# Cross-attention and quantized FFN on one core: scores and skip on fp16 pairs instead of fp32r pairs, with the scaling this needs

## The reference, cut to what matters

```python
def ln(x):                       # over the 1024 positions of a channel
    return (x - mean(x)) / sqrt(var(x) + 1e-5)
def xattn(u, c):                 # u: 128x1024, c: 128x256
    q, k, v = Wq @ u, Wk @ c, Wv @ c
    p = softmax(q.T @ k / sqrt(128))         # 1024 x 256
    return Wskip @ u + v @ p.T               # 128 x 1024
def ffn(u):                      # w: 1024x1024 from 4-bit weights
    return u @ w + bias
x = x + xattn(ln(x), ctx)
x = x + ffn(ln(x))
```

## Time and profile before

| | us |
|---|---|
| median of the three timed runs | 526.82 (526.39 to 528.74) |
| the profiled execution, its own time | 526.57 |
| its span in the trace | 524.6 |
| PE busy | 496.9 |
| POOL busy | 470.8 |
| DVE busy | 427.5 |
| ACT busy | 372.7 |

### The profile page before, as it was taken

The page is one execution under the profiler, slowest core; times in us unless marked ns, Lnnn a source line. Parts: engine busy times, 40 slices in busy tenths (PEclk is TensorE's granted clock), DMA queues, the critical chain, the costliest instruction groups (busy, mean ns, idle before and its releaser), DMA issues.

```text
span 524.6 us, 9213 instructions
## 1 busy us (share of the span) xinstructions
PE 496.9 (95%) x2668; PEld 302.8 (58%) x2668; DVE 427.5 (82%) x981; ACT 372.7 (71%) x844; POOL 470.8 (90%) x717
## 2 busy tenths in 40 slices
...
DMA packets 227059, 92.65 MB, mean 177 GB/s; under 512 B 209472, under 2 KB 214080, under 8 KB 227008
## 3 DMA queue, kind: packets, MB, share of 16 engines
...
q10 hardware_dynamic: 720, 0.14, 0.1%
...
## 4 chain that ended last, share of the span: by engine, by line
PE 86%; POOL 7%; DVE 2%; DMA 2%; issue 1%; ACT 1%; POOLq 0%; SPq 0%
PE ps_y L924 41%; PE ps_e L889 15%; PE ps_o L919 14%; PE ps_o L915 8%; PE ps_kv L900 3%; PE ps_y L928 3%; PE ps_kv L902 2%; POOL sb_prob L255 2%; POOL sb_xc_lo L270 1%; DMA sb_xnt_lo<-sb_xn_lo 1%; DMA sb_x<-in_x_dram 1%; POOL sb_xn_lo L302 1%; ACT sb_prob L480 1%; DVE sb_st L596 0%; ACT sb_wf L512 0%
## 5 line engine op out<-in xcount | busy, mean ns | idle before, releaser
L924 PE MATMUL ps_y<-sb_wf,sb_xnt_hi 128*128 128x512 f16 x512 | 192.1, 380 | 4.4 <-DMA sb_xnt_lo<-sb_xn_lo 3.4
L924 PE MATMUL ps_y<-sb_wf,sb_xnt_lo 128*128 128x512 f16 x512 | 192.0, 379 | 0.0
L480 ACT ACTIVATE sb_prob<-ps_e,sb_neg_max 128x256 f32<-128x256 f32 x256 | 118.3, 470 | 57.2 <-DVE sb_neg_max L659 57.2
L255 POOL TENSOR_SCALAR sb_prob<-sb_prob,sb_rsum 128x256 f32<-128x256 f32 x256 | 122.7, 492 | 15.2 <-DVE sb_rsum L664 15.0
L668 DVE TENSOR_TENSOR sb_p_lo<-sb_prob,sb_p_hi 128x1024 f16<-128x1024 f32 x64 | 78.3, 1223 | 48.8 <-ACT sb_p_hi L489 48.8
L889 PE MATMUL ps_e<-sb_k_hi,sb_xc_hi 128*128 128x256 f32 x256 | 90.8, 355 | 10.4 <-DVE sb_k_lo L647 5.7
L249 POOL TENSOR_TENSOR sb_o<-sb_prod,sb_x 128x512 f32<-128x512 f32 x63 | 80.6, 1279 | 7.0 <-DVE sb_prod L702 7.0
L924 PEld LDWEIGHTS ps_y<-sb_wf,sb_xnt_hi 128*128 128x128 f16 x512 | 49.9, 98 | 63.8 <-DMA sb_xnt_lo<-sb_xn_lo 4.3
L659 DVE TENSOR_REDUCE sb_neg_max<-ps_e 128x2 f32<-128x512 f32 x128 | 84.8, 681 | 1.6 <-PE ps_e L889 1.2
L924 PEld LDWEIGHTS ps_y<-sb_wf,sb_xnt_lo 128*128 128x128 f16 x512 | 50.0, 98 | 56.7
L489 ACT ACTIVATE sb_p_hi<-sb_prob 128x1024 f16<-128x1024 f32 x64 | 67.4, 1053 | 19.8 <-issue 15.5
...
## 6 DMA issues: line engine op xcount, KB each, us to landing
...
sb_pt_hi<-sb_p_hi SPq DMA_TRANSPOSE x64, 3.0
sb_pt_lo<-sb_p_lo SPq DMA_TRANSPOSE x64, 2.8
...
sb_xnt_hi<-sb_xn_hi SPq DMA_TRANSPOSE x32, 2.8
```

The lines of the kernel that those rows point to most:

```text
L255: last = pool.tensor_scalar(prob[:, j, t, :], prob[:, j, t, :], rsum[:, j, t:t + 1], P_SCALE, ALU.mult, ALU.mult)
L480: done = act.activation(prob[:, j, t, :], ps_e[j % 2][:, t, :], ACT.Exp, bias=neg_max[:, j, t:t + 1], accum_out=esum[:, j, t:t + 1])
L924: pe.matmul(ps_y[h][:, :], xnt_p[s][:, q % 2, kt, :], wf[:, kt, h * HALF:(h + 1) * HALF], start=kt == 0 and s == 0, stop=False)
```

## The change

It does this:

- The pairs of the scores and of the skip product become fp16 (`xc`, `k`, `wsk`). fp16 needs operands in range, so the first layernorm is applied in full, scaled to 1024: `inverse_std1` on POOL gets a second operation behind the power, `nb1` = -mean x inverse deviation, and ACT's `centre` uses `nb1` and `rstd1` as bias and scale pointers.
- The keys get a scale per batch: a second one-column matmul (`bound`) beside the one for the values gives a bound on the keys; DVE's `range_scales` makes both scales in three operations in place of the four of `value_scale`, and waits for the one-column matmuls instead of the key and value matmuls behind them.
- The key scale has to come out of the scores: `exps` gets a small ACT operation ahead of each chunk (`neg_top`, the row maxima times the scale, two elements per partition) for which the exponentials wait, and the exponentials get a scale pointer beside the bias pointer that they have.
- In the run-in the norms of the weights take one more reduction on DVE, the scaling of the weights moves from DVE to POOL, `key_bound` is added on DVE, the first `centre` is done in halves behind `nb1`, and `centre(1)` moves behind the exponentials of two chunks.

```diff
-        xc_hi, xc_lo = (sb(n, [P, 3, N], F32R) for n in ("xc_hi", "xc_lo"))
-        k_hi, k_lo = (sb(n, [P, 2, M], F32R) for n in ("k_hi", "k_lo"))
+        xc_hi, xc_lo = (sb(n, [P, 3, N], F16) for n in ("xc_hi", "xc_lo"))
+        k_hi, k_lo = (sb(n, [P, 2, M], F16) for n in ("k_hi", "k_lo"))
-        wsk_hi, wsk_lo = (sb(n, [C, 3, C], F32R) for n in ("wsk_hi", "wsk_lo"))
+        wsk_hi, wsk_lo = (sb(n, [C, 3, C], F16) for n in ("wsk_hi", "wsk_lo"))
...
             def inverse_std1(m):
                 pool.wait_ge(ve1_done, m + 1)
-                if ran(m, 2):
-                    pool.wait_ge(kvlo_done, m - 1)
-                pool.tensor_tensor(rstd1[:, m % 2:m % 2 + 1], ve1[:, :], neg_half[:, :],
-                                   ALU.pow).then_inc(rstd1_done, 1)
+                if ran(m, 1):
+                    pool.wait_ge(xc_done, m)
+                pool.tensor_tensor(rstd1[:, :], ve1[:, :], neg_half[:, :], ALU.pow).then_inc(rstd1_done, 1)
+                pool.wait_ge(rstd1_done, m + 1)
+                pool.tensor_scalar(nb1[:, :], mv1[:, 0:1], rstd1[:, :], -1.0, ALU.mult,
+                                   ALU.mult).then_inc(nb1_done, 1)
...
             def centre(n):
-                act.wait_ge(mv1_done, n + 1)
+                act.wait_ge(nb1_done, n + 1)
                 if ran(n, 1):
                     act.wait_ge(xclo_done, n)
-                act.activation(xc[:, :], x_sb[:, n % 4, :], ACT.Identity, bias=mv1[:, 0:1],
-                               scale=-1.0).then_inc(xc_done, 1)
+                act.activation(xc[:, :], x_sb[:, n % 4, :], ACT.Identity, bias=nb1[:, :],
+                               scale=rstd1[:, :]).then_inc(xc_done, 1)
...
             def exps(b, j):
                 act.wait_ge(max_done[j], b + 1)
                 if ran(b, 1):
                     act.wait_ge(plo_done[j // 2], b)
+                top = t_scale[:, b % 3, 1:2]
+                act.activation(neg_top[:, j, :], neg_max[:, j, :], ACT.Copy, scale=top).then_inc(top_done, 1)
+                act.wait_ge(top_done, CHUNKS * b + j + 1)
                 for t in range(TPC):
-                    done = act.activation(prob[:, j, t, :], ps_e[j % 2][:, t, :], ACT.Exp,
-                                          bias=neg_max[:, j, t:t + 1], accum_out=esum[:, j, t:t + 1])
+                    done = act.activation(prob[:, j, t, :], ps_e[j % 2][:, t, :], ACT.Exp, scale=top,
+                                          bias=neg_top[:, j, t:t + 1], accum_out=esum[:, j, t:t + 1])
                 done.then_inc(exp_done[j], 1)
...
             def run_in():
-                centre(0)
+                first_centre(0)
                 first_centred_hi(0)
                 keys_hi(0)
+                first_centre(1)
                 first_centred_hi(1)
                 keep_projections()
-                centre(1)
                 exps(0, 0)
                 exps(0, 1)
+                centre(1)
                 centred_hi(1)
...
-            def value_scale(n):
-                dve.wait_ge(kv_done, n + 1)
-                dve.tensor_scalar(t_scale[:, :], ps_m[:, HALF - 1:HALF], TINY, 1.0 / V_TOP, ALU.max,
-                                  ALU.mult).then_inc(t_step, 1)
-                dve.wait_ge(t_step, 4 * n + 1)
-                dve.reciprocal(v_scale[:, :], t_scale[:, :]).then_inc(t_step, 1)
-                dve.tensor_scalar(o_scale[:, n % 3:n % 3 + 1], t_scale[:, :], w_inv[:, :], None,
-                                  ALU.mult).then_inc(t_step, 1)
-                dve.wait_ge(t_step, 4 * n + 3)
-                dve.wait_ge(rstd1_done, n + 1)
-                dve.tensor_scalar(sk_scale[:, :], v_scale[:, :], rstd1[:, n % 2:n % 2 + 1], P_SCALE, ALU.mult,
+            def range_scales(n):
+                dve.wait_ge(bound_done, n + 1)
+                if n == 0:
+                    dve.wait_ge(floors_made, 2)
+                    dve.wait_ge(w_step, 5)
+                t = t_scale[:, n % 3, :]
+                dve.tensor_tensor(t, (ps_o[0] if n == 0 else ps_m)[:, HALF - 2:HALF], floors[:, :],
+                                  ALU.max).then_inc(t_step, 1)
+                dve.wait_ge(t_step, 3 * n + 1)
+                dve.reciprocal(t_inv[:, n % 2, :], t).then_inc(t_step, 1)
+                dve.tensor_scalar(o_scale[:, n % 3:n % 3 + 1], t_scale[:, n % 3, 0:1], w_inv[:, :], None,
                                   ALU.mult).then_inc(t_step, 1)
...
+            def bound(n, to):
+                pe.wait_ge(amax_done, n + 1)
+                peak = amax[:, n % 2:n % 2 + 1]
+                pe.matmul(to[:, HALF - 2:HALF - 1], top_inv[:, :], peak, start=True, stop=True)
+                pe.matmul(to[:, HALF - 1:HALF], kmax_row[:, :], peak, start=True, stop=True).then_inc(bound_done, 1)
...
             def keys_values(n):
                 pe.wait_ge(ctx_loaded[n % 2], nth(n, 2))
-                pe.wait_ge(amax_done, n + 1)
                 if ran(n, 1):
                     pe.wait_ge(kvlo_done, n)
-                pe.matmul(ps_m[:, HALF - 1:HALF], ones[:, :], amax[:, n % 2:n % 2 + 1], start=True, stop=True)
                 if n > 1:
+                    bound(n, ps_m)
                     pe.matmul(ps_kv[:, 0:M], proj[:, KEY, :], ctx_sb[:, n % 2, :], start=True, stop=True)
```

More of the change, by code:

```diff
@@ L97, in xattn_ffn_program @@
         mv1, mv2 = (sb(n, [P, 2]) for n in ("mv1", "mv2"))
-        rstd1 = sb("rstd1", [P, 2])
-        ve1, ve2, rstd2, nb2, rs2 = (sb(n, [P, 1]) for n in ("ve1", "ve2", "rstd2", "nb2", "rs2"))
+        ve1, rstd1, nb1, ve2, rstd2, nb2, rs2 = (sb(n, [P, 1]) for n in ("ve1", "rstd1", "nb1", "ve2", "rstd2", "nb2", "rs2"))
         ps_e = [pb(f"e{k}", [P, TPC, M]) for k in range(2)]
@@ L269, in centred_lo @@
                 cols = slice(h * HALF, (h + 1) * HALF)
-                last = pool.tensor_tensor(xc_lo[:, n % 3, cols], xc[:, cols], xc_hi[:, n % 3, cols].bitcast(F32),
+                last = pool.tensor_tensor(xc_lo[:, n % 3, cols], xc[:, cols], xc_hi[:, n % 3, cols],
                                           ALU.subtract)
@@ L364, in run_in @@
                 inverse_std1(0)
+                scale_weights()
                 zero_point_quotient()
```

111 lines of the change are left out of this document (65 added, 46 removed).

## The result

The changed kernel takes 550.96 us (median of 4 runs, 550.40 to 552.34) against 527.57 for the kernel before beside it (526.39 to 528.74): 1.045 times as long, 95% interval 1.041 to 1.048. The forecast said slower, at 543 with an upper end of 551; the measured time stands at that end. The profiled execution took 551.24, its span is 549.3.

What follows compares the result with a forecast made beforehand. It took PE to set the 15.22 us step, with a DVE, POOL and ACT loop close behind that would grow to 15.7. From 526.57 us, +13.4 for 28 steps, +2.5 run-in, +0.5 end: 543; range 522 to 551.

Steps and rivals of the forecast that it cites:

- the run-in: Start of the kernel, up to the FFN's start: 2.5 us longer, between 1 and 4.
- The step was right, 15.7: Steady step per batch: grows from 15.22 to 15.7 us, 28 times, +13.4 us in all.
- the ring: DVE, POOL and ACT waiting on each other in turn, from one `probs_lo(b, 1)` to the next: 15.22 us before the change.
- the loop: The same cycle through DVE, POOL and ACT: 14.91 us without PE, forecast at 15.45 to 15.95 after the change.
- the 0.31 us wait: DVE at `value_scale`, waiting for PE's key and value matmuls: the cycle's only slack, gone after the change.
- the middle that I took: 15.7 us a step, between 15.91 if `probs_lo(b, 0)` goes before `nb2` and about 15.5 if `nb2` goes first.
- The small costs: Per chunk on ACT, 0.31 us for the small operation and 0.18 for pointers on two exponentials; score matmuls at 0.108.
- The lock: A two-input DVE instruction and a POOL one reading SBUF exclude each other; the first to issue delays the other.
- PE's saving arrives: Rival: ACT's added costs are at most 0.1 us a chunk, PE's 14.92 us step holds, 521 us; chance 0.18.
- POOL becomes the bound: Rival: `nb1` costs 0.75 us and `xc_lo` gains nothing, step 16.2 or more, 557 us; chance 0.07.
- The last steps: End of the kernel: the last step's cycle adds 0.5 us.

Runs made afterwards that it cites:

- `wait_only`: The kernel before with POOL's product of mean and inverse deviation added and ACT's centring waiting for it, result unused: 533.90 us, ratio 1.012.
- `no_top`: The changed kernel without the small ACT operation and without the exponentials' scale pointer, softmax of unscaled scores: 521.39 us, ratio 0.988.
- `hi_first`: The changed kernel with POOL's third-batch power moved earlier, chunk 3 normalised before the second layernorm, and ACT's `probs_hi(b, 1)` before `apply_norm2`: 557.28 us, ratio 1.057.
- `dve_top`: The changed kernel with the scaled row maximum made on DVE instead of ACT, and POOL's third-batch power ahead of the zero-point remainder: 583.58 us, ratio 1.105.
- `halves_only`: The kernel before with only the score and skip pairs in fp16, unscaled, so low halves keep fewer digits: 516.16 us, ratio 0.979.
- `power_first`: The changed kernel with POOL's power and product for the third batch moved ahead of the zero-point remainder: 547.48 us, ratio 1.038.

## Why the forecast was right and wrong

**The step that failed is the run-in**: "1.1 + 2 x 0.49 + some 0.4", 2.5 us where 9.0 came: 6.5 of the 8 us that the forecast lacks. I counted that the first keys wait for the power and the product, and that the second centring stands behind two longer chunks. I did not follow the new wait to the third batch, whose power stands on POOL behind the zero-point work, and I took from the earlier trace rows that POOL had no gap there, when the change itself makes gaps: ACT waits for POOL (2.87 us), and POOL then for ACT's exponentials (2.99, the row at 31.82). `wait_only` shows 6.2 us for the wait by itself in the kernel before. In `no_top`, without the costs on ACT, the run-in is 5.2 us longer than before (first `sb_o` row at 61.74), so ACT's costs have 3.8 of the 9.0, where I had 2 x 0.49. The granted clock of TensorE is low in stretches of both run-ins (0.50 from 35 to 40 us before, 0.54 from 45 to 50 us after); what that costs there, no run shows.

**The step was right, 15.7, but partly by luck.** The row maxima of chunks 1 and 2 start 5.03 us into the ring (412.57 to 417.60), not 5.37: the loop held more slack than the 0.31 us wait that I took for all of it, and without PE and ACT's costs it takes about 14.4, where my terms make 14.7 (14.91 less the 0.2 saved on DVE). Of this lead 0.20 us is left at `probs_lo(b, 0)`, 11.92 us into the ring (396.84 to 408.76) for 12.12. And the two instructions did not split the difference: `probs_lo(b, 0)` went first, which I had priced at 15.91. Less 0.20, that is the 15.71 measured; the middle that I took is the same number for another reason. By the `sb_o` rows the step before is 15.18 and not 15.22, so the 28 steps cost 14.8 us for 13.4.

**The small costs held.** The small operation takes 0.29 us (0.30 forecast), an exponential 0.56 where it took 0.47 (0.088 forecast), score matmuls 0.109 apart (0.108). The profile has a mean of 560 ns for the exponential after and 470 before. The Trainium skill's page ScalarE: Activation LUTs, section What ACT_TABLE_LOAD costs, prices a pointer at 93 ns; the 90 ns here agree. PE's waits ahead of chunk 3's scores are 0.31 to 0.61 us in the steady steps, 0.61 in about half of them; I had asked for 0.6 or more.

**The lock** decides as the forecast's reading of the Trainium skill's page SBUF — State Buffer, section Who interferes with whom, had it: the two exclude each other and the first to issue keeps the other waiting. The trace agrees for `nb2`, which ends 0.12 to 0.14 us after the low half in the kernel before, the changed kernel and the three that lack one or both costs. POOL first, which the earlier trace rows did not have, is now shown: `hi_first` has the low half 0.80 us longer behind a sum that had started 0.34 us earlier, and `dve_top` has an operation of two elements, with one tile and a pointer for inputs, held to the end of a POOL instruction that had started 0.10 or 0.29 us earlier. It is not so for every pair. POOL's power on one element starts 0.06 us ahead of the low half in the kernel before (403.33),

```profile
403.27 0.55 POOL L279 TENSOR_TENSOR sb_rstd<-sb_ve,sb_neg_half 128x1 f32<-128x1 f32 x1
```

and neither holds up the other: 0.55 us and 1.21, as in the kernels where they lie further apart.

**The rivals.** "PE's saving arrives" decides where I put it, between no cost and the pointer's: 14.87 in `halves_only` and `no_top`, 15.01 with the pointer alone. "POOL becomes the bound" fell for this kernel (`no_top`: the same POOL work, 14.87), and `nb1` takes the 0.27 us that I had taken for it. The last steps cost 0.95 for 0.5. TensorE's granted clock falls there, as told below, and in `power_first`, where it doesn't, they take 43.2 us from the 29th sum on, for 44.0 in the changed kernel and 43.1 in the kernel before; that points to the clock, but doesn't show it.
